# A second chunk that comes in halves, and casts moved to GpSimd, at the head of a graph layer

## The chip, the cores and the metric

The kernel runs on one core of one Trainium2 chip. The metric is the device time of one execution in microseconds (us). Each kernel was run several times and the median is compared.

## The reference

The inputs are x (8192 x 256, float32), a mostly empty adj (8192 x 8192, float32) and a weight (256 x 256, float32). One layer is computed:

```python
bw = sign(weight)
ba = maximum(sign(x), 0)
xw = ba @ bw.T                      # 8192 x 256
out = relu(adj @ xw)                # 8192 x 256, sum over 8192
result = layernorm(x + out)         # over the 256 features
```

Nearly all arithmetic and nearly all bytes (268 MB of adj) are in `adj @ xw`.

## The kernel before, in words

**Blocks, chunks, units.** The 8192 rows of adj are cut into 16 blocks of 512 rows. The sum over 8192 columns is cut into 8 chunks of 1024 columns. A chunk of one block is 2 MB and has 4 units, so a block has 32 units and the kernel 512. The units are numbered through: units 0 to 3 are the first chunk, 4 to 7 the second, unit 8 begins the third. TensorE needs the summed index on the partitions, so each unit is turned first.

**What happens to a unit.** VectorE turns it by 32x32 blocks (`turn`, L392), ScalarE makes a rounded copy `hi` of it (`make_hi`, L279), and then `lo`, the rest, is the turned unit minus `hi`. In "P" units GpSimd makes `lo` (L259, `turned` in SBUF); in "V" units VectorE does (`make_lo`, L396, `turned_v` in PSUM). Units 0, 1, 4 and 7 are V, units 2, 3, 5, 6, 8 and 9 are P. TensorE then multiplies `hi` and `lo` with `xw` and sums in PSUM (`use_unit`).

**The head: how xw is made.** During the first block xw is made too, in 16 groups of 4 steps of 128 rows of x; a chunk needs two groups, a group serves two units. For group g: x is cast to bf16 (`first_cast` L359 on VectorE for groups 0 and 1, `cast` L267 on ScalarE from group 2), TensorE transposes it (`turn_step`, L520), VectorE makes the step 0 or 1 (`make_step`, L365), TensorE multiplies with the signs of the weight (`make_xw`, L530), and the product is copied to SBUF (VectorE for group 0, L445; ScalarE's `copy_xw`, L272, for the others). TensorE's order is written out: transposes of group 0, product 0, transposes of group 1, then unit 0, product 1, transposes 2, unit 1, unit 2, product 2, transposes 3, units 3 and 4, product 3, transposes 4, units 5 and 6, and so on. A unit of a group waits until that group's product is copied.

**The first chunk in halves.** Units 0 to 3 hold half of the block's rows (256) and four steps, and not all 512 rows and two steps, so that unit 0 can start when half of the chunk has landed. Their products are 16 matmuls of 256 columns (L548) in place of 8 of 512 (L554). From unit 4 on a chunk is turned only when all of it has landed.

**The queues.** SyncE and ScalarE issue all loads, each two of the four quadrants of 32 partitions, each on its own queue. The issues of ScalarE stand in its program between its computing instructions: after `make_hi(n)` come the issues of x (L182) and adj (L168) that `x_at` and `issue_at` put at unit n, and after these, in the same pass, `copy_xw` and `cast`. The order on each queue is: weight, x for group 0, first half of chunk 0, x for group 1, its second half, then the two quadrants of x and of adj for the second chunk. Then, one quadrant at a time, x, adj, x, adj for each later chunk. SyncE issues the same at `units_turned` thresholds.

**What a first chunk's bytes are.** A chunk's x is 1.05 MB, a chunk of adj 2.10 MB, the weight 0.26 MB. Half of a first chunk is 1.05 MB, one group's x is 0.52 MB.

Of the kernel before, what the change touches and what calls it, by code (L numbers as in the profile page):

```python
# [5 lines left out]
Q = 32  # L6
G = P // Q
# [3 lines left out]
def build(nc, x, adj, w, out):  # L11
# [5 lines left out]
    NT = MB // Q  # L17
# [3 lines left out]
    SLOTS = 4  # L21
    CH = 8
    KC = N // CH
    KG = KC // G
    KB = KG // Q
# [3 lines left out]
    UPC = KB // UK  # L29
# [7 lines left out]
    GROUPS = CH * KB // GK  # L37
    UPG = GK // UK
    STEP_BUFS = 2
    BACK_AT = 4  # L40


# [15 lines left out]
        return before[kinds[n]][n]  # L58


    X_PIECES = [(0, GK), (GK, GK)] + [(c * KB, KB) for c in range(1, CH)]

    def piece_of_group(g):
        return g if g < KB // GK else g * GK // KB + 1

    adj_v = adj.rearrange("(b t i) (c g k) -> b c g i t k", t=NT, i=Q, c=CH, g=G)
    x_turn = x.rearrange("(c g b j) d -> c g j b d", c=CH, g=G, b=KB)
# [5 lines left out]
    with ctx:  # L73
# [3 lines left out]
        def sem(name):  # L77
            return ctx.enter_context(nc.semaphore(name))
# [39 lines left out]

        w_loaded = sem("w_loaded")
        x_loaded = [sem(f"x_loaded{i}") for i in range(len(X_PIECES))]  # L120
        halves_loaded = [sem(f"halves_loaded{i}") for i in range(2)]
        adj_loaded = [sem(f"adj_loaded{s}") for s in range(SLOTS)]
        rows_loaded = sem("rows_loaded")
        rows_stored = sem("rows_stored")
# [4 lines left out]
        signs_made = sem("signs_made")  # L129
        signs_turned = sem("signs_turned")  # L130
        signs_copied = sem("signs_copied")
        first_casts = sem("first_casts")
        casts_made = sem("casts_made")
        casts_turned = sem("casts_turned")
        steps_made = sem("steps_made")
# [27 lines left out]
        def raw_view(ch):  # L163
            return raw[:, ch % SLOTS, :].rearrange("p (t k) -> p t k", t=NT)
# [5 lines left out]

        def start_half(eng, i, quadrants):

            t0, t1 = i * NT // 2, (i + 1) * NT // 2
            for g in quadrants:
                eng.dma_start(raw_view(0)[g * Q:(g + 1) * Q, t0:t1],
                              adj_v[0, 0, g, :, t0:t1]).then_inc(halves_loaded[i], 16)

        def start_x(eng, i, quadrants):
            first, count = X_PIECES[i]
# [5 lines left out]


        def issue_at(ch, half):
            early = 4 + 2 * half if ch < CH else max(CH + 3 - ch, 0) + half
            return max(UPC * (ch - SLOTS + 1) + early, 0)

        def x_at(c, half):
            return max(UPC * c - 9 + 2 * half, 0)

        @block.sync
        def _(sp):
            sp.dma_start(w_sb[:, 0], w_rows[:, 0]).then_inc(w_loaded, 16)
            for i in range(2):
                start_x(sp, i, LOWER)
                start_half(sp, i, LOWER)

            def load_chunk(ch):
                if ch >= SLOTS:

                    sp.wait_ge(units_turned, (ch - SLOTS + 1) * UPC)
                start_chunk(sp, ch, LOWER)

            def store_rows(b):
                sp.wait_ge(blocks_done, b + 1)
                sp.dma_start(out_rows[b], rows[:]).then_inc(rows_stored, 16)

            def load_rows(b):
                if b == 0:

                    sp.wait_ge(xw_made, GROUPS)
                else:
                    sp.wait_ge(rows_stored, b * 16)
                sp.dma_start(rows[:], x_rows[b]).then_inc(rows_loaded, 16)

            start_x(sp, 2, LOWER)
            load_chunk(1)  # L220
            for c in range(2, CH):

                for half in range(2):
                    sp.wait_ge(units_turned, x_at(c, half) + 1)
                    start_x(sp, c + 1, LOWER[half:half + 1])
                    sp.wait_ge(units_turned, issue_at(c, half) + 1)
                    start_chunk(sp, c, LOWER[half:half + 1])
            for b in range(1, NBLK):
                for c in range(CH):
                    load_chunk(b * CH + c)  # L230
                    if c == 2 and b >= 2:
                        store_rows(b - 2)
                    if c == 3:
                        load_rows(b - 1)
            store_rows(NBLK - 2)
            load_rows(NBLK - 1)
            for b, ms in PIECES:
                if b == NBLK - 1:
                    sp.wait_ge(blocks_done, NBLK)
                else:  # L240
                    sp.wait_ge(last_piece_done, 1)
                sp.dma_start(out_rows[NBLK - 1, :, ms[0]:ms[-1] + 1],
                             rows[:, ms[0]:ms[-1] + 1]).then_inc(rows_stored, 16)
            sp.wait_ge(rows_stored, (NBLK - 1 + len(PIECES)) * 16)

        @block.gpsimd
        def _(pool):
            pool.memset(eps[:], EPS).then_inc(eps_set, 1)
            pool.memset(ident[:], 0.0).then_inc(zeroed, 1)
            pool.memset(ident_b[:], 0.0).then_inc(zeroed, 1)  # L250
            pool.wait_ge(zeroed, 2)
            for m in (ident, ident_b):
                pool.affine_select(out=m[:], in_=m[:], compare_op=ALU.not_equal, fill=1.0, base=0,
                                   pattern=[[-1, P]], channel_multiplier=1).then_inc(idents_made, 1)
            for n in range(UNITS):
                if kinds[n] == "P":

                    pool.wait_ge(his_made, n + 1)
                    pool.tensor_tensor(lo[:, n % RING], turned[:, ordinal(n) % TP], hi[:, n % RING].bitcast(f32),  # L259
                                       ALU.subtract).then_inc(p_los_made, 1)  # L260

        @block.scalar
        def _(act):
# [47 lines left out]
            start_half(act, 0, UPPER)  # L311
            act.wait_ge(eps_set, 1)
            act.activation(warm[:], eps[:], ACT.Copy)
            start_x(act, 1, UPPER)
            start_half(act, 1, UPPER)
            start_x(act, 2, UPPER)
            start_chunk(act, 1, UPPER)
            for n in range(UNITS):
                make_hi(n)
                for c in range(2, CH):  # L320
                    for half in range(2):
                        if n == x_at(c, half):
                            start_x(act, c + 1, UPPER[half:half + 1])
                for ch in range(2, NCHUNK):

                    for half in range(2):
                        if n == issue_at(ch, half):
                            start_chunk(act, ch, UPPER[half:half + 1])
                if n < UB:
                    g = n // UPG  # L330
                    if n % UPG and g >= 1:
                        copy_xw(g)
                    if n % UPG and g + 2 < GROUPS:
                        cast(g + 2)
                else:
                    ending(n // UB - 1, n % UB)
            act.wait_ge(relus_turned, (NBLK - 1) * MT)

# [11 lines left out]
        def _(dve):  # L350
# [3 lines left out]
            dve.scalar_tensor_tensor(out=sign_w[:], in0=w_sb, scalar=0.0, in1=w_neg,  # L354
                                     op0=ALU.is_gt, op1=ALU.subtract).then_inc(signs_made, 1)

            def first_cast(n):
                dve.wait_ge(x_loaded[n], G * 16)
                dve.tensor_copy(cast_x[:, n], x_sb[:, n * GK:(n + 1) * GK]).then_inc(first_casts, 1)  # L359

            def make_step(n):
                dve.wait_ge(casts_turned, n + 1)
                if n >= 2:
# [2 lines left out]

            def turn(n):
                ch, u = n // UPC, n % UPC
                if ch == 0:
                    if u < 2:  # L370
                        dve.wait_ge(halves_loaded[u], G * 16)
                elif u == 0:

                    dve.wait_ge(adj_loaded[ch % SLOTS], (ch // SLOTS + (ch % SLOTS > 0)) * G * 16)
                if kinds[n] == "P":
                    dst = turned[:, ordinal(n) % TP]
                    if ordinal(n) >= TP:
                        dve.wait_ge(p_los_made, ordinal(n) - TP + 1)
                else:
                    dst = turned_v  # L380
                    if n == 0:
                        dve.wait_ge(signs_copied, 1)
                    else:
                        dve.wait_ge(v_los_made, ordinal(n))
                src = raw[:, ch % SLOTS, :].rearrange("p (t k j) -> p k t j", t=NT, j=Q)
                if ch == 0:

                    g, t0 = u // UPG, u % UPG * NT // 2
                    uk, src = GK, src[:, g * GK:(g + 1) * GK, t0:t0 + NT // 2]
                else:  # L390
                    uk, src = UK, src[:, u * UK:(u + 1) * UK]
                dve.transpose(dst.rearrange("p (k t j) -> p k t j", k=uk, j=Q), src).then_inc(units_turned, 1)  # L392
# [43 lines left out]
                    make_shift(b, whole)  # L436


            first_cast(0)
            dve.wait_ge(signs_turned, 1)  # L440
            dve.tensor_copy(sign_wT[:], ps_wT).then_inc(signs_copied, 1)
            make_step(0)
            turn(0)
            dve.wait_ge(xw_made, 1)
            dve.tensor_copy(xw[:, 0:GK], ps_xw).then_inc(xw_copied, 1)  # L445
            first_cast(1)

            make_lo(0)
            make_step(1)
# [53 lines left out]
        def _(pe):  # L503
# [5 lines left out]
            last.then_inc(signs_turned, 1)  # L509

            def turn_step(n):
                if n < STEP_BUFS:
                    pe.wait_ge(first_casts, n + 1)
                else:
                    pe.wait_ge(casts_made, n - STEP_BUFS + 1)
                if n >= 2:
                    pe.wait_ge(steps_made, n - 1)
                for k in range(GK):
# [15 lines left out]
            def use_unit(n):  # L534
# [21 lines left out]
                                     start=(step == 0 and part is hi),  # L556
                                     stop=(step == last_step and part is lo))

                if n < UPC:
                    for k in range(GK):  # L560
                        for a in range(DH):
                            for part in (hi, lo):
# [114 lines left out]
```

## Time and profile before

| | |
|---|---|
| median of 3 runs | 992.87 us (991.89 to 993.97) |
| profiled execution, its own time | 991.81 us |
| span of its instructions | 989.9 us |
| TensorE busy | 972.1 us, 98% |
| GpSimd, VectorE, ScalarE busy | 839.8, 847.3, 613.5 us |
| loads and stores over the span | 297 GB/s read |

The span lies inside the profiled execution, 1.9 us shorter than its time. Engines are named PE (TensorE matmul), PEld (its weight loads), DVE (VectorE), ACT (ScalarE), POOL (GpSimd) and SP (SyncE); ACTq and SPq are the DMA issues that ACT's and SP's sequencers carry out. L12 is line 12 of the kernel. Times in rows are us from the span's start.

### The profile page before, as it was taken

How to read it: one execution, taken by the hardware profiler on the slowest of the kernel's cores; microseconds unless marked ns; L12 is line 12 of the kernel's file. 1: busy time of each engine (PE TensorE's matmuls, PEld its weight loads, DVE VectorE, ACT ScalarE, POOL GpSimd, SP SyncE). 2: the span in 40 equal slices, each digit the busy share in tenths (PEclk: the TensorE clock that was granted, in tenths of full speed). 3: DMA queues.
4: the chain of work that ended last, by engine and by line, in shares of the span. 5: the costliest groups of instructions: out<-in, count | busy, mean ns of one | idle time of the engine just before them, and what ended most of it. 6: DMA issues, size and time to landing. Idle time of an engine off the chain costs nothing.

```text
span 989.9 us, 12378 instructions
## 1 busy us (share of the span) xinstructions
PE 972.1 (98%) x4548; PEld 806.7 (81%) x4548; DVE 847.3 (86%) x879; ACT 613.5 (62%) x655; POOL 839.8 (85%) x360
## 2 busy tenths in 40 slices
PE   5999999999999999999999999999999999999997
PEld 4888888888888888888888888888888888888886
DVE  5868998989888898988989898898988989898894
ACT  3877675665656566565665656566565656656562
POOL 2567998988889889898998889899888998889893
PEclk9999999999999999999999999999999999999999
DMA  9999999999999999999999999999999999999971
GB/s 306 348 341 318 322 318 323 278 312 299 321 294 291 296 312 317 288 312 306 288 297 303 324 282 308 304 315 314 288 319 287 313 295 305 319 281 308 307 204 43
DMA packets 296428, 294.69 MB, mean 298 GB/s; under 512 B 9392, under 2 KB 296368, under 8 KB 296368
## 3 DMA queue, kind: packets, MB, share of 16 engines
q1 hardware_dynamic: 156640, 155.34, 57.2%
q10 hardware_dynamic: 139728, 138.56, 49.7%
q8 instruction: 36, 0.59, 0.3%
q14 instruction: 24, 0.20, 0.1%
HBM read 285.47 MB, written 8.39 MB: 297 GB/s over the span
## 4 chain that ended last, share of the span: by engine, by line
PE 97%; DVE 1%; DMA 1%; issue 0%; ACT 0%; ACTq 0%; DVEq 0%
PE ps L554 93%; PE ps L628 1%; PE ps L530 1%; DMA raw<-in_adj_dram 1%; PE ps L520 1%; PE ps L592 1%; PE ps L548 0%; ACTq L182 0%; DVE ps L392 0%; ACT hi L279 0%; DVE stats L404 0%; DVE rows L481 0%; PE ps L616 0%; DVE xw L445 0%; DVE lo L396 0%
## 5 line engine op out<-in xcount | busy, mean ns | idle before, releaser
L259 POOL TENSOR_TENSOR lo<-turned,hi 128x1024 fp32r<-128x1024 f32 x351 | 838.7, 2412 | 135.1 <-ACT hi L279 131.1
L554 PE MATMUL ps<-hi,xw 128*128 128x512 f32 x2016 | 787.1, 390 | 0.0
L554 PE MATMUL ps<-lo,xw 128*128 128x512 f32 x2016 | 784.7, 389 | 0.0
L279 ACT ACTIVATE hi<-turned 128x1024 fp32r<-128x1024 f32 x351 | 372.3, 1062 | 255.8 <-PE ps L554 173.6
L554 PEld LDWEIGHTS ps<-hi,xw 128*128 128x128 f32 x2016 | 378.5, 188 | 78.0
L554 PEld LDWEIGHTS ps<-lo,xw 128*128 128x128 f32 x2016 | 378.5, 188 | 77.9
L392 DVE STREAM_TRANSPOSE turned<-raw 128x1024 f32<-128x1024 f32 x351 | 425.1, 1218 | 0.0
L396 DVE TENSOR_TENSOR lo<-ps,hi 128x1024 fp32r<-128x1024 f32 x161 | 196.5, 1220 | 106.3 <-ACT hi L279 106.3
L279 ACT ACTIVATE hi<-ps 128x1024 fp32r<-128x1024 f32 x161 | 165.1, 1026 | 89.9 <-PE ps L554 77.2
L392 DVE STREAM_TRANSPOSE ps<-raw 128x1024 f32<-128x1024 f32 x161 | 196.2, 1219 | 3.8 <-DMA raw<-in_adj_dram 3.8
L296 ACT ACTIVATE rows<-rows,shift,rstd 128x256 f32<-128x256 f32 x62 | 36.3, 586 | 0.6 <-DVE shift L415 0.6
L365 DVE TENSOR_SCALAR rows<-ps 128x1024 bf16<-128x1024 bf16 x16 | 10.9, 679 | 14.1 <-PE ps L520 14.1
L404 DVE BATCH_NORM_STATS2 stats<-rows 128x6 f32<-128x256 f32 x64 | 22.4, 412 | 0.1
L272 ACT ACTIVATE xw<-ps 128x1024 fp32r<-128x1024 f32 x15 | 15.4, 1024 | 10.5 <-PE ps L530 8.4
L530 PE MATMUL ps<-sign_wT,rows 128*128 128x256 bf16 x128 | 18.1, 288 | 0.9 <-DVE rows L365 0.9
L400 DVE TENSOR_TENSOR rows<-ps,rows 128x1024 f32<-128x1024 f32 x15 | 18.0, 1199 | 0.0
L530 PEld LDWEIGHTS ps<-sign_wT,rows 128*128 128x128 bf16 x128 | 11.8, 103 | 6.2 <-issue 4.5
L267 ACT ACTIVATE relu<-x_sb 128x1024 bf16<-128x1024 f32 x14 | 14.7, 1050 | 2.6 <-DMA x_sb<-in_x_dram 2.6
L288 ACT ACTIVATE relu<-ps 128x512 f32<-128x512 f32 x30 | 16.0, 584 | 0.0
L628 PEld LDWEIGHTS ps<-ident,relu 128*128 128x128 f32 x120 | 14.0, 140 | 2.0
L628 PE MATMUL ps<-ident,relu 128*128 128x128 f32 x120 | 15.5, 272 | 0.0
L520 PE MATMUL ps<-ident_b,relu 128*128 128x128 bf16 x128 | 10.6, 230 | 3.5 <-DVE relu L359 3.5
(38 smaller groups left out, 109.8 us busy)
## 6 DMA issues: line engine op xcount, KB each, us to landing
raw<-in_adj_dram SPq DMA_DIRECT2D x254, 512.0 KB, 11.1
raw<-in_adj_dram ACTq DMA_DIRECT2D x254, 512.0 KB, 12.0
rows<-in_x_dram SPq DMA_DIRECT2D x16, 512.0 KB, 10.7
out_dram<-rows SPq DMA_DIRECT2D x15, 512.0 KB, 15.8
x_sb<-in_x_dram SPq DMA_DIRECT2D x14, 256.0 KB, 10.2
x_sb<-in_x_dram ACTq DMA_DIRECT2D x14, 256.0 KB, 11.9
raw<-in_adj_dram SPq DMA_DIRECT2D x4, 256.0 KB, 7.0
raw<-in_adj_dram ACTq DMA_DIRECT2D x4, 256.0 KB, 7.8
```

The lines of the kernel that those rows point to most:

```text
L259: pool.tensor_tensor(lo[:, n % RING], turned[:, ordinal(n) % TP], hi[:, n % RING].bitcast(f32), ALU.subtract).then_inc(p_los_made, 1)
L279: act.activation(hi[:, n % RING], src, ACT.Copy).then_inc(his_made, 1)
L288: act.activation(relu[:, a], acc[b % 2][a], ACT.Relu).then_inc(relus_made, 1)
L296: done = act.activation(rows[:, m], rows[:, m], ACT.Identity, bias=shift[:, m:m + 1], scale=rstd[:, m:m + 1])
L392: dve.transpose(dst.rearrange("p (k t j) -> p k t j", k=uk, j=Q), src).then_inc(units_turned, 1)
L396: dve.tensor_tensor(lo[:, n % RING], turned_v[:, :], hi[:, n % RING].bitcast(f32), ALU.subtract).then_inc(v_los_made, 1)
L400: dve.tensor_tensor(rows[:, ms], back[:, ms], rows[:, ms], ALU.add).then_inc(sums_made, 1)
L404: dve.bn_stats(stats[:, m], rows[:, m]).then_inc(stats_made, 1)
L520: last = pe.transpose(ps_xT[n % 2][:, k, i], cast_x[:, n % STEP_BUFS, k, i * P:(i + 1) * P], ident_b[:])
L530: last = pe.matmul(ps_xw[:, k], step_xT[:, n % 2, k, i], sign_wT[:, i], start=(i == 0), stop=(i == DH - 1))
L554: return pe.matmul(acc[b % 2][a], xw[:, step, a * P:(a + 1) * P], part[:, n % RING, k * MB:(k + 1) * MB], start=(step == 0 and part is hi) ...
L628: last = pe.transpose(back[:, m, a * P:(a + 1) * P], relu[:, a, m * P:(m + 1) * P], ident[:])
```

## The change

The second chunk is loaded in halves of its rows too, and its x in two groups of 0.52 MB. Units 4 to 7 become units of half the rows and four steps, like units 0 to 3. Group 0 is cast by VectorE as before, groups 1 and 2 are cast by GpSimd, the others by ScalarE. Product 0 is copied by ScalarE. ScalarE copies products 0 to 3 right after `make_hi` of units 0, 2, 4 and 6 (the products before: at units 3, 5, 7), and both `copy_xw` and `cast` now come ahead of the DMA issues of the same unit. The last half of the second chunk is issued after the first unit is turned, and the quadrants of later chunks one unit later than before.

```diff
+    EARLY_CASTS = 3
...
-    X_PIECES = [(0, GK), (GK, GK)] + [(c * KB, KB) for c in range(1, CH)]
+    HALVED = 2
+    X_PIECES = [(g * GK, GK) for g in range(HALVED * UPC // UPG)] + [(c * KB, KB) for c in range(HALVED, CH)]
...
         def issue_at(ch, half):
-            early = 4 + 2 * half if ch < CH else max(CH + 3 - ch, 0) + half
+            early = 5 + 2 * half if ch < CH else max(CH + 3 - ch, 0) + half
...
         def x_at(c, half):
-            return max(UPC * c - 9 + 2 * half, 0)
+            return UPC * (c - HALVED) + 2 * half
...
-            for i in range(2):
+            for i in range(2 * HALVED):
                 start_x(sp, i, LOWER)
-                start_half(sp, i, LOWER)
+                if i < 2 * HALVED - 1:
+                    start_half(sp, i, LOWER)
+
+            sp.wait_ge(units_turned, 1)
+            start_half(sp, 2 * HALVED - 1, LOWER)
...
-            start_x(sp, 2, LOWER)
-            load_chunk(1)
...
+            for g in range(1, EARLY_CASTS):
+                pool.wait_ge(x_loaded[g], G * 16)
+                if g >= STEP_BUFS:
+                    pool.wait_ge(casts_turned, g - STEP_BUFS + 1)
+                pool.tensor_copy(cast_x[:, g % STEP_BUFS], x_sb[:, g * GK:(g + 1) * GK]).then_inc(pool_casts, 1)
...
-            start_x(act, 1, UPPER)
-            start_half(act, 1, UPPER)
-            start_x(act, 2, UPPER)
-            start_chunk(act, 1, UPPER)
+            for i in range(1, 2 * HALVED):
+                start_x(act, i, UPPER)
+                if i < 2 * HALVED - 1:
+                    start_half(act, i, UPPER)
             for n in range(UNITS):
                 make_hi(n)
+                if n < UB:
+                    g = n // UPG
+                    if n % UPG == (0 if g < HALVED * UPC // UPG else 1):
+                        copy_xw(g)
+                    if n % UPG and EARLY_CASTS <= g + 2 < GROUPS:
+                        cast(g + 2)
+                if n == 0:
+                    start_half(act, 2 * HALVED - 1, UPPER)
...
-                if n < UB:
-                    g = n // UPG
-                    if n % UPG and g >= 1:
-                        copy_xw(g)
-                    if n % UPG and g + 2 < GROUPS:
-                        cast(g + 2)
...
-                if ch == 0:
+                if ch < HALVED:
                     if u < 2:
-                        dve.wait_ge(halves_loaded[u], G * 16)
+                        dve.wait_ge(halves_loaded[2 * ch + u], G * 16)
...
-            first_cast(0)
+            dve.wait_ge(x_loaded[0], G * 16)
+            dve.tensor_copy(cast_x[:, 0], x_sb[:, 0:GK]).then_inc(first_cast, 1)
...
             turn(0)
-            dve.wait_ge(xw_made, 1)
-            dve.tensor_copy(xw[:, 0:GK], ps_xw).then_inc(xw_copied, 1)
-            first_cast(1)
...
-                if n < UPC:
+                if n < HALVED * UPC:
                     for k in range(GK):
```

## Rows read from the trace of the kernel before

**Rows 1.** The page: busy time by engine, and the chain that ended last.
```profile
PE 972.1 (98%) x4548; PEld 806.7 (81%) x4548; DVE 847.3 (86%) x879; ACT 613.5 (62%) x655; POOL 839.8 (85%) x360
...
PE 97%; DVE 1%; DMA 1%; issue 0%; ACT 0%; ACTq 0%; DVEq 0%
```
**Rows 2.** Waits of PE: us in total, times, longest.
```profile
PE ps L548 <- ACT xw L272: 2.2, 1, 2.2
```
**Rows 3.** Busy time by stretch: length, PE, PEld, DVE, ACT, POOL, PEclk, DMA, GB/s.
```profile
80.00:970.00 890.00, 890.00 (x4012) 737.75 (x4011) 783.97 (x803) 556.99 (x596) 794.03 (x333) 1.00 1.09 301
```
**Rows 4.** Timeline of ACT: start, us, instruction, idle before it.
```profile
15.97 1.74 ACTq L182 DMA_DIRECT2D x_sb<-in_x_dram  x1
...
19.44 3.36 ACTq L182 DMA_DIRECT2D x_sb<-in_x_dram  x1
...
22.85 1.02 ACT L272 ACTIVATE xw<-ps 128x1024 fp32r<-128x1024 f32 x1 [2.08 <-issue]
...
29.49 1.06 ACT L267 ACTIVATE relu<-x_sb 128x1024 bf16<-128x1024 f32 x1 [1.26 <-DMA x_sb<-in_x_dram]
...
30.45 1.04 ACT L279 ACTIVATE hi<-turned 128x1024 fp32r<-128x1024 f32 x1
```
**Rows 5.** The chain that ended last, in order of time: start, us, what.
```profile
26.10 0.89 PE ps L530 x8
26.99 0.45 PE ps L520 x8
27.44 1.96 PE ps L548 x16
29.40 1.84 PE ps L554 x8
```
**Rows 6.** Timeline of DVE, early.
```profile
12.26 0.68 DVE L359 CAST relu<-x_sb 128x1024 bf16<-128x1024 f32 x1
12.86 1.22 DVE L396 TENSOR_TENSOR lo<-ps,hi 128x1024 fp32r<-128x1024 f32 x1
...
33.30 1.25 DVE L392 STREAM_TRANSPOSE turned<-raw 128x1024 f32<-128x1024 f32 x1
```
**Rows 7.** Timeline of POOL, early.
```profile
1.35 0.29 POOL L253 TENSOR_SCALAR_AFFINE_SELECT ident<-ident 128x128 f32<-128x128 f32 x1 [0.24 <-POOL ident_b L250]
...
19.90 4.71 POOL L259 TENSOR_TENSOR lo<-turned,hi 128x1024 fp32r<-128x1024 f32 x2 [18.01 <-ACT hi L279]
...
31.57 2.39 POOL L259 TENSOR_TENSOR lo<-turned,hi 128x1024 fp32r<-128x1024 f32 x1 [2.14 <-ACT hi L279]
35.72 4.76 POOL L259 TENSOR_TENSOR lo<-turned,hi 128x1024 fp32r<-128x1024 f32 x2 [1.76 <-ACT hi L279]
```
**Rows 8.** Issue to landing: x of group 1 (issued 3.1 to 3.6), x at 16.0, adj at 17.9.
```profile
DMA to landing us min/median/max: 6.5/6.8/7.7
...
DMA to landing us min/median/max: 12.5/13.0/13.5
...
DMA to landing us min/median/max: 15.4/15.4/15.4
```
**Rows 9.** Timeline of PE: units 0 and 1's work, unit 6's and 8's first matmul.
```profile
14.23 0.55 PE L548 MATMUL ps<-hi,xw 128*128 128x256 f32 x1 [0.19 <-DVE lo L396]
...
19.56 0.36 PE L548 MATMUL ps<-hi,xw 128*128 128x256 f32 x1
...
34.31 0.40 PE L554 MATMUL ps<-hi,xw 128*128 128x512 f32 x1
...
39.37 0.40 PE L554 MATMUL ps<-hi,xw 128*128 128x512 f32 x1
```
**Rows 10.** Busy time by stretch, from the start to three landings (columns as Rows 3).
```profile
0.00:17.80 17.80, 8.09 (x45) 6.44 (x45) 10.76 (x13) 3.53 (x4) 1.12 (x9) 1.00 0.95 289
0.00:23.49 23.49, 12.01 (x76) 9.86 (x76) 13.05 (x15) 7.13 (x8) 4.71 (x11) 1.00 0.99 303
0.00:29.45 29.45, 17.54 (x125) 15.23 (x126) 19.00 (x21) 11.54 (x12) 8.23 (x12) 1.00 1.01 312
```

More of the change, by code:

```diff
@@ L58, in ordinal, with piece_of_chunk @@
         return before[kinds[n]][n]
-    X_PIECES = [(0, GK), (GK, GK)] + [(c * KB, KB) for c in range(1, CH)]
+    HALVED = 2
+    X_PIECES = [(g * GK, GK) for g in range(HALVED * UPC // UPG)] + [(c * KB, KB) for c in range(HALVED, CH)]
     def piece_of_group(g):
-        return g if g < KB // GK else g * GK // KB + 1
+        return [i for i, (first, count) in enumerate(X_PIECES) if first <= g * GK < first + count][0]
+    def piece_of_chunk(c):
+        return X_PIECES.index((c * KB, KB))
     adj_v = adj.rearrange("(b t i) (c g k) -> b c g i t k", t=NT, i=Q, c=CH, g=G)
@@ L120, in build @@
         x_loaded = [sem(f"x_loaded{i}") for i in range(len(X_PIECES))]
-        halves_loaded = [sem(f"halves_loaded{i}") for i in range(2)]
+        halves_loaded = [sem(f"halves_loaded{i}") for i in range(2 * HALVED)]
         adj_loaded = [sem(f"adj_loaded{s}") for s in range(SLOTS)]
@@ L131, in build @@
         signs_copied = sem("signs_copied")
-        first_casts = sem("first_casts")
+        first_cast = sem("first_cast")
+        pool_casts = sem("pool_casts")
         casts_made = sem("casts_made")
@@ L171, in start_half @@
         def start_half(eng, i, quadrants):
-            t0, t1 = i * NT // 2, (i + 1) * NT // 2
+            ch, t0 = i // 2, i % 2 * NT // 2
             for g in quadrants:
-                eng.dma_start(raw_view(0)[g * Q:(g + 1) * Q, t0:t1],
-                              adj_v[0, 0, g, :, t0:t1]).then_inc(halves_loaded[i], 16)
+                eng.dma_start(raw_view(ch)[g * Q:(g + 1) * Q, t0:t0 + NT // 2],
+                              adj_v[0, ch, g, :, t0:t0 + NT // 2]).then_inc(halves_loaded[i], 16)
         def start_x(eng, i, quadrants):
@@ L217, in load_rows @@
                 sp.dma_start(rows[:], x_rows[b]).then_inc(rows_loaded, 16)
-            start_x(sp, 2, LOWER)
-            load_chunk(1)
-            for c in range(2, CH):
+            for c in range(HALVED, CH):
                 for half in range(2):
                     sp.wait_ge(units_turned, x_at(c, half) + 1)
-                    start_x(sp, c + 1, LOWER[half:half + 1])
+                    start_x(sp, piece_of_chunk(c), LOWER[half:half + 1])
                     sp.wait_ge(units_turned, issue_at(c, half) + 1)
@@ L313, in _ @@
             act.activation(warm[:], eps[:], ACT.Copy)
-            start_x(act, 1, UPPER)
-            start_half(act, 1, UPPER)
-            start_x(act, 2, UPPER)
-            start_chunk(act, 1, UPPER)
+            for i in range(1, 2 * HALVED):
+                start_x(act, i, UPPER)
+                if i < 2 * HALVED - 1:
+                    start_half(act, i, UPPER)
             for n in range(UNITS):
                 make_hi(n)
-                for c in range(2, CH):
+                if n < UB:
[6 more added lines that the diff above has]
+                    start_half(act, 2 * HALVED - 1, UPPER)
+                for c in range(HALVED, CH):
                     for half in range(2):
                         if n == x_at(c, half):
-                            start_x(act, c + 1, UPPER[half:half + 1])
+                            start_x(act, piece_of_chunk(c), UPPER[half:half + 1])
                 for ch in range(2, NCHUNK):
@@ L328, in _ @@
                             start_chunk(act, ch, UPPER[half:half + 1])
-                if n < UB:
-                    g = n // UPG
-                    if n % UPG and g >= 1:
-                        copy_xw(g)
-                    if n % UPG and g + 2 < GROUPS:
-                        cast(g + 2)
-                else:
+                if n >= UB:
                     ending(n // UB - 1, n % UB)
@@ L355, in _ @@
                                      op0=ALU.is_gt, op1=ALU.subtract).then_inc(signs_made, 1)
-            def first_cast(n):
-                dve.wait_ge(x_loaded[n], G * 16)
-                dve.tensor_copy(cast_x[:, n], x_sb[:, n * GK:(n + 1) * GK]).then_inc(first_casts, 1)
             def make_step(n):
@@ L368, in turn @@
                 ch, u = n // UPC, n % UPC
-                if ch == 0:
+                if ch < HALVED:
                     if u < 2:
-                        dve.wait_ge(halves_loaded[u], G * 16)
+                        dve.wait_ge(halves_loaded[2 * ch + u], G * 16)
                 elif u == 0:
-                    dve.wait_ge(adj_loaded[ch % SLOTS], (ch // SLOTS + (ch % SLOTS > 0)) * G * 16)
+                    dve.wait_ge(adj_loaded[ch % SLOTS], (ch // SLOTS + (ch % SLOTS >= HALVED)) * G * 16)
                 if kinds[n] == "P":
@@ L385, in turn @@
                 src = raw[:, ch % SLOTS, :].rearrange("p (t k j) -> p k t j", t=NT, j=Q)
-                if ch == 0:
+                if ch < HALVED:
                     g, t0 = u // UPG, u % UPG * NT // 2
@@ L511, in turn_step @@
             def turn_step(n):
-                if n < STEP_BUFS:
-                    pe.wait_ge(first_casts, n + 1)
+                if n == 0:
+                    pe.wait_ge(first_cast, 1)
+                elif n < EARLY_CASTS:
+                    pe.wait_ge(pool_casts, n)
                 else:
-                    pe.wait_ge(casts_made, n - STEP_BUFS + 1)
+                    pe.wait_ge(casts_made, n - EARLY_CASTS + 1)
                 if n >= 2:
```

## The prediction

> **What bounds the kernel now.** The page comes first. TensorE is busy 972.1 of 989.9 us, and 97% of the chain that ended last is its own work [rows 1]. The stretches say where the rest is: from 80 to 970 us it is busy 890.00 of 890.00 us [rows 3]. So an edit of the first 40 us can only move the moment from which TensorE never waits again. I look for that moment in TensorE's waits. After its first unit there is one wait, 2.2 us, for ScalarE's copy of product 1 [rows 2]. ScalarE's timeline shows why the copy was late: an issue of x began at 19.44, held ScalarE's sequencer for 3.36 us, and the copy behind it started at 22.85 after 2.08 us of "issue" [rows 4]. The change plainly removes this wait, since the copy now comes ahead of the issues. The question is what is late next.
>
> **What lies close behind the wait.** Two more things on ScalarE and GpSimd run in the shadow of those 2.2 us. ScalarE's cast of group 4 waited for x of the third chunk until 29.49. `make_hi` of unit 6 stands behind this cast in ScalarE's program and began at 30.45 [rows 4]. GpSimd's `lo` of unit 6 ran from 31.57 for 2.39 us, to 33.96 [rows 7]. TensorE began unit 6 at 34.31 [rows 9]. So unit 6 had 0.35 us in hand, less than a sixth of the wait that goes. This chain begins at a landing, and the change leaves cast 4 where it was, behind `make_hi(5)` and ahead of `make_hi(6)`.
>
> **When that landing comes.** Here I compare bytes moved with bytes queued up to a landing. At 17.8 us 289 GB/s had moved 5.14 MB (x of the second chunk ends at 0.26 + 3.15 + 1.05 = 4.46 MB of the order). At 23.49, when the second chunk was in, it was 7.12 MB (6.55 in the order). At 29.45 it was 9.19 MB; x of the third chunk ends at 6.55 + 0.52 + 1.05 + 0.52 = 8.65 MB [rows 10]. The lead is 0.68, 0.57 and 0.54 MB: landings follow bytes moved, at (9.19 - 7.12) / 5.96 us = 347 GB/s between the last two. The delay from issue to landing is no constant: 7.7 us for an x issue at 3.6, 13.5 for one at 16.0 [rows 8], as the backlog grew. The change reorders bytes only within the second chunk; from x of the third chunk on the order is x, adj, x, adj as before. So x of the third chunk still lands at 29.5, provided no queue runs empty. By the same rule the new pieces land so: first half of the second chunk (4.98 MB + 0.6) at 19.1, its second half at 23.5.
>
> **The change part by part.**
>
> *Copy 0 and cast 1 leave VectorE.* `make_lo(0)` then waits only for `make_hi(0)`, which ends at 12.2; it started at 12.86 behind a cast of 0.68 us [rows 6]. Gain 0.6 us. Copy 0 on ScalarE takes 1.02 us [rows 4], done by 13.3, beside it.
>
> *Casts 1 and 2 on GpSimd.* The trace shows no cast there. From below: 0.29 us, an operation with one input on 128 columns; from above: 2.40 us, half of 4.76, the operation with two inputs on the same 1024 columns [rows 7]. I take the upper, which has the right size. x of group 1 has landed by 3.6 + 7.7 = 11.3 [rows 8]. So the cast ends at 13.7, the transposes of group 1 take about 1.1 us at the slow start, and unit 0 starts at 14.9 (at 13.6, set by `lo`, if the cast takes less than about 1.2). It was 14.23 [rows 9]. From the first matmul of unit 0 to that of unit 1 took 19.56 - 14.23 = 5.33 us, with product 1 and the transposes of group 2 [rows 9]. A half unit is 1.96, a product 0.89, the transposes 0.45 [rows 5]. Without waits unit 6 would start after that, units 1 to 5 (9.80), products 2 and 3 and transposes 3 and 4 (2.68): 17.8 us after unit 0, at 31.4 to 32.7. Both ends lie ahead of 33.96, so the cast's price is hidden.
>
> *Second chunk in halves.* Unit 4 no longer waits for the whole chunk, but `make_lo(4)` stands behind `turn(5)`, which waits for the second half at 23.5. It ends near 25.9, as needed. Price: 1.96 - 1.84 = 0.12 us for each of units 4 to 7 [rows 5]. Units 4 and 5 pay it while TensorE would wait anyway, units 6 and 7 on the path: +0.24 us.
>
> *The wait that takes the place of the old one.* Transposes 4 need cast 4, which ends at 29.49 + 1.06 = 30.55 [rows 4]; then 0.45 + 1.96 bring unit 6 to 33.0 at the earliest, and its `lo` to 33.96. So unit 6 starts at 34.0, not 34.31: -0.31 us. TensorE will wait 0.3 to 1.3 us before transposes 4 and 1 us before unit 6, where it waited 2.2 us earlier.
>
> *Issues one unit later, and behind copies.* Behind the waiting copies and casts on ScalarE stand the issues of its queue. The tightest is x of the fourth chunk and then adj, the latter behind cast 4, at about 29.5. By then ScalarE's queue has been given 5.0 MB and has moved about half of 9.19, 4.6, or a little less. It has 0.4 to 0.6 MB left, over 2 us of work at half of 347 GB/s, so it stays fed, and I cost this at nothing. If this cover went, adj of the fourth chunk would be late; its units are three further on. `turn(8)` ran at 33.30 with adj issued at 17.9 and 15.4 us to landing, so on landing [rows 6, 8]; that too stays.
>
> *Sum.* -0.31 + 0.24 = -0.07, say -0.1 us at unit 8 (39.3 for 39.37) and from there to the end. The profiled execution's 991.81 (span 989.9 and 1.9 around it) would become 991.7. It lay 1.06 under the median of the runs, so the median becomes 992.87 - 0.1 = **992.8 us**.
>
> **The rivals.** 0.2% (2.0 us) is about what a measurement of this kernel can tell from no change.
>
> *Landings come earlier.* SyncE's half of that x landed after 12.5 us, at 28.5, ScalarE's at 29.5 [rows 8]. Were they even, or less held up by full queues, x could land 0.5 to 1 us earlier and unit 6 with it. Unit 8 bounds this. Its `lo` ends at 35.72 + 2.4 = 38.1 [rows 7] and follows the landing of adj at 33.3; unit 8 started at 39.37 [rows 9]. So with adj unmoved at most 1.25 us come: 991.6 to 992.3, still "same". Chance 0.12. With both landings early by over a microsecond the whole wait would come back: 34.31 - 31.4 - 0.24 = 2.7 us, 990.2. Chance 0.07; the steady 347 GB/s speaks against it.
>
> *The other side: the delay from issue counts.* ScalarE's second x issue of the third chunk was at 15.97 [rows 4]. Now it stands behind copy 1, which waits for product 1 on TensorE, at 18.4 to 19.9. If 13.5 us from issue still held, x would land at 31.9 to 33.4 and unit 6 would start 2.4 to 3.9 us later than at 34.0: 995.2 to 996.7. It decides from a landing at 31.6 on. Against it stand the bytes [rows 10]. It needs an empty queue. Chance 0.05.
>
> *GpSimd's cast is slow.* Unit 0 may start up to 34.0 - 17.8 = 16.2 without harm, so the cast may take 16.2 - 1.1 - 11.3 = 3.8 us. Beyond it each microsecond costs one. At three times a `lo` (7.2 us) that is +3.3: 996.2. Against it: the first `lo` of all began right when `hi` was there, and the first two took 4.71 us, later two 4.76 [rows 7]; no first use was dear. Chance 0.04. The Trainium skill (GPSIMD Engine Reference, section Instruction dispatch) says that the first call to a freshly loaded GpSimd kernel pays about 6 us more. An estimate by that page is a cast of 2.4 + 6 = 8.4 us, and then 4.5 us slower. By that rule the first `lo` should have shown it too; the trace has no such gap, so I leave it its small chance.
>
> **Chances.** Forecast (within a few tenths of 992.8) 0.72; earlier x alone 0.12; everything earlier 0.07; later landings 0.05; slow cast 0.04. Faster by over 0.2%: 0.07. Within: 0.72 + 0.12 = 0.84. Slower: 0.09. The range reaches down to the case of the earlier x with some spread of the median, 991.2, and up by a microsecond, the spread of the runs shown, 993.9.
>
> **What would show it.** Right: TensorE's wait for L272 gone, two new waits near 30 and 33 us, on L267 and on L259; cast 4 waiting for x until about 29.5; unit 8 starting near 39.3; GpSimd's casts between 0.3 and 2.4 us. Wrong: cast 4 starting before 28.5 or after 30, any wait of TensorE beyond 40 us, a GpSimd cast over 3.8 us, or a queue that runs empty.

## The result, and the profile after

The changed kernel takes 1004.31 us (median of 6 runs, 998.12 to 1011.44), the kernel before 993.42 us (median of 6, 991.89 to 994.34). The ratio is 1.0113, with a 95% interval of 1.0067 to 1.0159. It is 1.1% slower, outside the range of the prediction, and its runs lie 13 us apart where those of before lie within 2.5 us; why they scatter so is not shown. Ratios here and below are of the means of the runs, the times are medians. The profiled execution took 1000.46 us, with a span of 998.7 us, so the rows below show one of the milder cases: 8.8 us more span.

Busy time by engine and the chain that ended last, on the page of the kernel after, answer to [rows 1]:

```profile
PE 974.7 (98%) x4580; PEld 807.9 (81%) x4580; DVE 845.7 (85%) x877; ACT 612.5 (61%) x655; POOL 841.9 (84%) x362
...
PE 90%; DMA 7%; issue 1%; DVE 0%; ACT 0%; POOL 0%; ACTq 0%; DVEq 0%; POOLq 0%
```

The busy time of TensorE is 2.6 us longer, and the other 6 us of the loss are waits. The halves explain a small part of the 2.6 us: e3 below keeps them and has 972.5 us. Where the rest comes from stays open. Transfers are 7% of the chain, where they were 1%. TensorE's waits from 0 to 110 us (engine, line, what it waited for, us in total, times, longest):

```profile
PE ps L533 <- ACT relu L281: 4.5, 5, 1.8
PE ps L567 <- POOL lo L273: 2.9, 3, 1.0
PE ps L533 <- POOL relu L268: 2.2, 1, 2.2
...
PE ps L567 <- ACT xw L286: 0.3, 1, 0.3
```

The wait of [rows 2] for the copy is gone, as the change intends. In its place TensorE waits five times for a cast of x on ScalarE and three times for a `lo` behind one. By unit 8, where the forecast stopped, little of the loss is there. Its first matmul starts at 39.89, against 39.37 before and 39.3 foretold:

```profile
39.89 0.40 PE L567 MATMUL ps<-hi,xw 128*128 128x512 f32 x1
```

ScalarE's timeline of the kernel after answers to [rows 4]:

```profile
23.80 0.32 ACTq L189 DMA_DIRECT2D x_sb<-in_x_dram  x1
25.00 1.06 ACT L293 ACTIVATE hi<-turned 128x1024 fp32r<-128x1024 f32 x1 [0.18 <-DVE turned L405]
29.99 1.06 ACT L281 ACTIVATE relu<-x_sb 128x1024 bf16<-128x1024 f32 x1 [3.93 <-DMA x_sb<-in_x_dram]
30.00 0.32 ACTq L175 DMA_DIRECT2D raw<-in_adj_dram  x1
30.47 0.39 ACTq L189 DMA_DIRECT2D x_sb<-in_x_dram  x1
30.95 1.04 ACT L293 ACTIVATE hi<-turned 128x1024 fp32r<-128x1024 f32 x1
...
40.45 1.06 ACT L281 ACTIVATE relu<-x_sb 128x1024 bf16<-128x1024 f32 x1 [1.74 <-DMA x_sb<-in_x_dram]
40.46 0.32 ACTq L175 DMA_DIRECT2D raw<-in_adj_dram  x1
...
52.37 1.06 ACT L281 ACTIVATE relu<-x_sb 128x1024 bf16<-128x1024 f32 x1 [2.80 <-DMA x_sb<-in_x_dram]
52.38 0.32 ACTq L175 DMA_DIRECT2D raw<-in_adj_dram  x1
```

Cast 4 waits until 29.99 (foretold: 29.5). Directly behind it, at 30.00, comes an adj issue that the kernel before made at 24.79, well ahead of its cast 4:

```profile
24.79 0.36 ACTq L168 DMA_DIRECT2D raw<-in_adj_dram  x1
```

Between the issues of 23.80 and 30.00 ScalarE issues nothing. The stretches of the kernel after (columns as in [rows 3]; the last number is GB/s) show what follows:

```profile
31.00:32.00 1.00, 0.90 (x12) 0.90 (x13) 0.24 (x1) 1.00 (x3) 0.00 (x0) 1.00 1.11 350
32.00:33.00 1.00, 1.00 (x11) 1.00 (x10) 0.45 (x1) 1.00 (x2) 0.93 (x1) 1.00 1.14 317
33.00:34.00 1.00, 0.68 (x6) 0.48 (x4) 0.93 (x1) 1.00 (x2) 1.00 (x1) 1.00 1.10 212
34.00:35.00 1.00, 0.39 (x3) 0.42 (x4) 1.00 (x2) 1.00 (x2) 0.46 (x1) 1.00 1.15 211
35.00:36.00 1.00, 1.00 (x11) 1.00 (x10) 1.00 (x2) 0.71 (x1) 0.21 (x1) 1.00 1.08 254
```

The rate falls from 350 to 211 GB/s, while the DMA share stays at 1.10 or more: that column alone would have hidden it. The queues of the kernel after (packets, MB, share of 16 engines) at 31 to 32, 33 to 34 and 35 to 36 us:

```profile
q10 hardware_dynamic: 181, 0.18, 56.0%
q1 hardware_dynamic: 174, 0.17, 55.1%
...
q1 hardware_dynamic: 196, 0.20, 104.2%
q10 hardware_dynamic: 13, 0.01, 6.3%
...
q10 hardware_dynamic: 127, 0.13, 54.9%
q1 hardware_dynamic: 129, 0.12, 53.6%
```

q10, by the times ScalarE's queue, runs all but dry after 32 us and flows again after 35. The two issues of 30.00 and 30.47 do not help it for about 5 us. SyncE's queue, with the other almost dry, moves 0.20 MB in a microsecond, where the two together move 0.35. Later SyncE's queue runs dry too: it issues nothing from 40.00 to 46.48, and from 49 to 51 us q1 moves 0.05 MB and q10 0.38. The rate stays low over most of block 0. From 55 to 65 us, first before and then after:

```profile
55.00:65.00 10.00, 10.00 (x65) 8.14 (x64) 6.94 (x8) 7.81 (x9) 7.03 (x4) 1.00 1.10 348
```

```profile
55.00:65.00 10.00, 9.00 (x53) 6.73 (x51) 6.46 (x6) 5.29 (x6) 6.61 (x3) 1.00 1.12 241
```

Five times in block 0 the same loop goes round. The chain of the kernel after, in order of time:

```profile
30.47 9.96 DMA x_sb<-in_x_dram
...
40.90 11.45 DMA x_sb<-in_x_dram
...
52.82 12.24 DMA x_sb<-in_x_dram
...
65.53 11.64 DMA x_sb<-in_x_dram
...
77.64 11.97 DMA x_sb<-in_x_dram
```

A cast waits for x; behind the cast stand the issue of the next adj and of the next x; that x lands 10 to 12 us later, and the next even cast waits for it. The even casts began at 29.99, then 40.45, 52.37, 65.08, 77.19 and 89.64: 59.65 us for five chunks, 11.9 each. In the kernel before cast 4 began at 29.49 and cast 14 at 79.09, without a wait for x, 49.6 us for the same five:

```profile
79.09 1.04 ACT L267 ACTIVATE relu<-x_sb 128x1024 bf16<-128x1024 f32 x1
```

### The profile page after: what moved, and what is told of

Read it like the earlier page. It is cut to its first block, busy times and chain, and to the rows that moved or that the text cites. A ratio compares the mean times of both kernels' runs of the same rounds, so it can differ in the third digit from the quotient of the medians.

```text
span 998.7 us, 12450 instructions
## 1 busy us (share of the span) xinstructions
PE 974.7 (98%) x4580; PEld 807.9 (81%) x4580; DVE 845.7 (85%) x877; ACT 612.5 (61%) x655; POOL 841.9 (84%) x362
## 3 DMA queue, kind: packets, MB, share of 16 engines
q10 hardware_dynamic: 139792, 138.56, 49.6%
## 4 chain that ended last, share of the span: by engine, by line
PE 90%; DMA 7%; issue 1%; DVE 0%; ACT 0%; POOL 0%; ACTq 0%; DVEq 0%; POOLq 0%
PE ps L567 88%; DMA x_sb<-in_x_dram 7%; PE ps L641 1%; PE ps L605 1%; PE ps L561 0%; PE ps L543 0%; ACT relu L281 0%; ACTq L175 0%; DVE stats L417 0%; PE ps L533 0%; DVE rows L492 0%; PE ps L629 0%; POOL relu L268 0%; ACT xw L286 0%; DVE mv L420 0%
## 5 line engine op out<-in xcount | busy, mean ns | idle before, releaser
L561 PE MATMUL ps<-hi,xw 128*128 128x256 f32 x64 | 17.6, 309 | 1.0 <-POOL lo L273 0.9
L561 PE MATMUL ps<-lo,xw 128*128 128x256 f32 x64 | 17.0, 299 | 0.0
L533 PEld LDWEIGHTS ps<-ident_b,relu 128*128 128x128 bf16 x128 | 8.6, 103 | 10.4 <-ACT relu L281 5.9
```

What stands on the lines that cost most here:

```text
L533: last = pe.transpose(ps_xT[n % 2][:, k, i], cast_x[:, n % STEP_BUFS, k, i * P:(i + 1) * P], ident_b[:])
L561: return pe.matmul(acc[b % 2][a][:, n0:n0 + MB // 2], xw[:, step, a * P:(a + 1) * P], part[:, n % RING, k * MB // 2:(k + 1) * MB // 2], st ...
```

## The experiments

Each run below leaves the computation whole. A is the theory of the dry queue behind a waiting cast, B is that the issues simply come a unit too late, C is that the halves cost it.

**e1: the kernel after with the issue times of before.**

```diff
-            early = 5 + 2 * half if ch < CH else max(CH + 3 - ch, 0) + half
+            early = 4 + 2 * half if ch < CH else max(CH + 3 - ch, 0) + half
...
-            return UPC * (c - HALVED) + 2 * half
+            return max(UPC * c - 9 + 2 * half, 0)
```

> The kernel after, with only the issue times of the kernel before (x and adj of later chunks one unit earlier). Theory A (ScalarE's issues stand behind a cast that waits for a landing, and its queue runs dry): one adj quadrant now comes ahead of cast 4, at about 24 us, but x and the next adj still stand behind it, at 30; the queue just runs out when they begin to flow, so part of the loss stays: 993 to 997 us. Theory B (the issues come one unit too late, wherever they stand): the whole loss goes, 992 to 993.5 us. Theory C (the halves of the second chunk, with their smaller transfers and matmuls, cost it): nothing changes, 1000 us or more.

Measured: 992.8 us against 993.6, ratio 0.9993 (0.9984 to 1.0001). The whole loss is gone, more than A as first put had allowed. This run alone fits B.

**e2: the kernel after with ScalarE's casts behind the issues of their unit.**

```diff
-                    if n % UPG and EARLY_CASTS <= g + 2 < GROUPS:
-                        cast(g + 2)
...
                         if n == issue_at(ch, half):
                             start_chunk(act, ch, UPPER[half:half + 1])
+                if n < UB and n % UPG and EARLY_CASTS <= g + 2 < GROUPS:
+                    cast(g + 2)
```

> The kernel after, with ScalarE's casts moved behind the issues of the same unit; the issue times stay one unit later. Theory A: ScalarE's queue no longer runs dry behind a waiting cast, 992 to 994 us. Theory B: the loss stays in most part, above 997 us. Theory C: 1000 us or more.

Measured: 993.19 against 993.6 us, ratio 1.0001 (0.9991 to 1.0011); one of the twelve runs took 997.48. Here every issue still comes a unit late, so B falls; and in e1 the issues still stand behind the casts, so the place alone is not enough either. What e1 and e2 share at cast 4 is one transfer: the first adj quadrant of the fourth chunk, 0.52 MB, is issued by ScalarE ahead of the cast. ScalarE's issue, first of e1 and then of e2:

```profile
24.88 0.32 ACTq L175 DMA_DIRECT2D raw<-in_adj_dram  x1
```

```profile
25.48 0.36 ACTq L175 DMA_DIRECT2D raw<-in_adj_dram  x1
```

The stretch of the dry queue, first of e1 and then of e2:

```profile
32.00:35.00 3.00, 2.07 (x18) 1.90 (x17) 2.46 (x3) 3.00 (x5) 2.39 (x1) 1.00 1.10 348
```

```profile
32.00:35.00 3.00, 2.07 (x18) 1.90 (x17) 2.37 (x3) 3.00 (x5) 2.39 (x1) 1.00 1.10 347
```

Theory A2: both moves together put that quadrant, and its like in each later chunk, behind the waiting cast.

**e3: both edits.** The diffs of e1 and e2 together.

> Both edits: issue times of the kernel before, and ScalarE's casts behind the issues of their unit; halves, GpSimd's casts and the early copies stay. Theories A and B: 992 to 993.3 us, equal to the kernel before or a few tenths under it, since x of the third chunk still lands near 29.5 us. Theory C: 1000 us or more.

Measured: 992.69 against 993.6 us, ratio 0.9999 (0.9984 to 1.0013); one of the eleven runs took 1000.68, and no profile shows why. Halves, GpSimd's casts and the early copies stay, and together they cost or bring at most 0.16%. C falls.

**e4: the kernel before with `copy_xw` ahead of the issues of its unit.**

```diff
                 make_hi(n)
+                if n < UB and n % UPG and n // UPG >= 1:
+                    copy_xw(n // UPG)
...
-                    if n % UPG and g >= 1:
-                        copy_xw(g)
```

> The kernel before, with only copy_xw moved ahead of the issues of its unit. By the chain of cast 4, make_hi(6) and lo(6), the wait of 2.2 us for the copy goes and all but 0.35 us of it comes back before unit 6: 0.3 us faster, 993.1 against 993.4. Rival, that the wait was the only one: 2.2 us faster. Theory A adds that an issue behind a copy that waits costs nothing as long as the queue holds several microseconds of work.

Measured: 993.07 against 993.6 us, ratio 0.9996 (0.9988 to 1.0005). The rival, that all 2.2 us are gained, lies outside the interval. This is the prediction's step from the copy to unit 6 by itself. First two rows of ScalarE's timeline in e4, then its chain at unit 6 (start, us, what):

```profile
20.82 1.00 ACT L272 ACTIVATE xw<-ps 128x1024 fp32r<-128x1024 f32 x1
...
30.16 1.06 ACT L267 ACTIVATE relu<-x_sb 128x1024 bf16<-128x1024 f32 x1 [2.17 <-DMA x_sb<-in_x_dram]
```

```profile
32.24 2.40 POOL lo L259
34.64 0.14 issue
34.78 2.08 PE ps L554 x8
```

Copy 1 runs at 20.82 in place of 22.85, and the 2 us come back whole: cast 4 waits for x, `lo` of unit 6 ends at 34.64 and TensorE begins the unit behind it.

**e5: the kernel before with the two moves of the change alone.** Issue times one unit later, ScalarE's `copy_xw` and `cast` ahead of the issues; no halves, no cast on GpSimd.

```diff
-            early = 4 + 2 * half if ch < CH else max(CH + 3 - ch, 0) + half
+            early = 5 + 2 * half if ch < CH else max(CH + 3 - ch, 0) + half
...
-            return max(UPC * c - 9 + 2 * half, 0)
+            return UPC * (c - 2) + 2 * half
...
                 make_hi(n)
+                if n < UB:
+                    g = n // UPG
+                    if n % UPG and g >= 1:
+                        copy_xw(g)
+                    if n % UPG and g + 2 < GROUPS:
+                        cast(g + 2)
```

> The kernel before, with two moves of the change alone: issues of later chunks one unit later, and ScalarE's copy and cast ahead of the issues of their unit. No halves in the second chunk, no cast on GpSimd. Theory A2 (these two together put one adj quadrant behind cast 4, from about 25 to 30 us, and ScalarE's queue needs it some 5 us before it is empty): the loss is there, 998 to 1010 us, with stretches near 210 GB/s. Theory C (halves): 993 us.

Measured: 1001.47 against 993.5 us, ratio 1.0073 (1.0049 to 1.0097). These two moves make a loss of this kind. Whether they make all of it isn't resolved, 0.73% for 1.13% with intervals that overlap. The profiled execution is the slowest of the six, 1004.77 us. Its queues from 33 to 35 us:

```profile
q1 hardware_dynamic: 412, 0.41, 106.3%
q10 hardware_dynamic: 30, 0.02, 6.9%
```

**e6: the kernel after with SyncE's issues one unit earlier.**

```diff
-                    sp.wait_ge(units_turned, x_at(c, half) + 1)
+                    sp.wait_ge(units_turned, max(x_at(c, half), 1))
...
-                    sp.wait_ge(units_turned, issue_at(c, half) + 1)
+                    sp.wait_ge(units_turned, max(issue_at(c, half), 1))
```

> The kernel after, with only SyncE's issues one unit earlier, ScalarE's unchanged. Theory A2 (ScalarE's queue runs out first, SyncE's only as a consequence): most of the loss stays, 998 us or more, and the first slow stretch is at 32 to 35 us as before. Theory B2 (both queues together are short): below 996 us.

Measured: 1002.06 against 993.5 us, ratio 1.0091 (1.0071 to 1.0111). Earlier issues on SyncE's queue do not help, while e2, which edits ScalarE's program alone, removes the loss: the cause is on ScalarE's. I had expected the slow stretch at 32 to 35 us as before. The slow stretch came about 1 us later (236 GB/s at 34 to 35 us, 199 at 35 to 36), with cast 4 at 31.50.

**e9: the kernel after with one single issue moved ahead of cast 4.**

```diff
+                    if n == issue_at(3, 0):
+                        start_chunk(act, 3, UPPER[0:1])
                     if n % UPG and EARLY_CASTS <= g + 2 < GROUPS:
                         cast(g + 2)
...
-                        if n == issue_at(ch, half):
+                        if n == issue_at(ch, half) and (ch, half) != (3, 0):
```

> The kernel after, with one single issue of ScalarE moved: the first adj quadrant of the fourth chunk comes ahead of cast 4 (near 25 us) and not behind it (30 us). The same stands behind casts 6, 8, 10, 12 and 14 still. Theory F (the first dry stretch starts it, and each late landing makes the next cast late and with it the next issues): ScalarE's queue holds a quadrant more at 30 us, the stretch of 32 to 35 us stays near 348 GB/s and most or all of the loss goes, 992 to 996 us. Theory G (each chunk makes its own dry stretch, whatever came before): only the first of six goes, 1000 us or more.

Measured: 999.27 against 993.7 us, ratio 1.0068 (1.0054 to 1.0082). The stretches of e9, columns as before:

```profile
32.00:35.00 3.00, 2.12 (x19) 1.92 (x16) 2.25 (x3) 3.00 (x4) 2.40 (x1) 1.00 1.10 347
42.00:44.00 2.00, 2.00 (x20) 1.68 (x19) 1.00 (x2) 1.14 (x2) 1.52 (x1) 1.00 1.11 223
```

The first dry stretch is gone with the one transfer, as A2 says. But the next comes at 42 us, behind cast 6. So a chunk makes its own (theory G), and the first is not what starts them all; F falls. The time lies between the two forecasts, 0.7 us under the 1000 of G. The loss is 0.68% for 1.13%, and the intervals overlap, so how much went with the one transfer is not resolved.

**e7: e3, and both quadrants of a chunk's x ahead of its adj.**

```diff
-            return max(UPC * c - 9 + 2 * half, 0)
+            return max(UPC * c - 9, 0)
...
+                sp.wait_ge(units_turned, x_at(c, 0) + 1)
+                start_x(sp, piece_of_chunk(c), LOWER)
                 for half in range(2):
-                    sp.wait_ge(units_turned, x_at(c, half) + 1)
-                    start_x(sp, piece_of_chunk(c), LOWER[half:half + 1])
```

> As e3 (old issue times, casts behind the issues), and both quadrants of a chunk's x issued ahead of its adj. If the bytes ahead of it set when x lands, x of the third chunk (7.6 MB and a lead of 0.6) lands near 26.5 us in place of 30, cast 4 holds nobody up, and unit 8 is bound by the landing of adj at 33.3 us: it starts 1 to 1.2 us ahead of the 39.37 us of the kernel before, 992.4 against 993.6 us. Rival, that the delay from issue counts: no gain, 993 us or more.

Measured: 991.81 against 993.5 us, ratio 0.9985 (0.9976 to 0.9994). Cast 4 no longer holds anybody up: it ran at 28.52 without a wait for x. The profile of e7 shows the new bound, and not the gain that I expected of it. Its chain:

```profile
18.70 15.06 DMA raw<-in_adj_dram
...
33.79 1.25 DVE turned L405
...
38.30 1.01 ACT xw L286
39.31 0.04 issue
39.35 2.11 PE ps L567 x8
```

adj of the third chunk lands at 33.8, and unit 8 starts at 39.35, as in the kernel before (39.37). The time is 0.15% lower all the same; this execution (991.87 us, beside 991.81 for that of the kernel before) is no witness for where that comes from, and it stays open.

**e8: e4, and both quadrants of a chunk's x ahead of its adj.** The same edit on the kernel before; no halves, no cast on GpSimd.

> As e4 (the kernel before with copy_xw first), and both quadrants of a chunk's x ahead of its adj; whole second chunk, no cast on GpSimd. It tells what the halves are worth once x comes early: unit 4 then still waits for the whole second chunk at 23.5 us and its lo, near 27 us, where TensorE could be there near 25; the gain against the kernel before is that of e7 or a few tenths of a microsecond more (no dearer matmuls): 992.2 to 992.8 us.

Measured: 991.7 against 993.5 us, ratio 0.9981 (0.9973 to 0.999). It is faster than the kernel before by 0.19%, more than I had expected, and no slower than e7, so the second chunk's halves and GpSimd's casts bring nothing that shows even then. Its profiled span is 989.1 us, 0.8 us under the 989.9 of before. The whole of it is there at unit 8, which starts here, in place of at 39.37:

```profile
38.56 0.40 PE L554 MATMUL ps<-hi,xw 128*128 128x512 f32 x1
```

This is the version to keep.

## Why the prediction was wrong

**Right.** What the change removes went, and the chain behind it was the right one: cast 4 at 29.99 (29.5 foretold), two new waits of TensorE, GpSimd's cast at 1.04 us (between 0.29 and 2.40). The 0.24 us put down for the halves are too small for these runs to show. The 0.3 us of gain at unit 6 did not come: it started at 34.61, with cast 4 half a microsecond late (34.31 before, 34.0 foretold). Two of the signs named for a wrong forecast did come: a queue that runs empty, and waits of TensorE beyond 40 us. The experiment e4 shows the step by itself: without the copy's wait unit 6 waits for its `lo`, and nothing is gained. The rule that landings follow bytes moved held roughly where both queues were full: when x of the third chunk had landed, ScalarE's queue had moved 4.56 MB before, 4.66 MB after and 4.80 MB in e6, where that was at 31.5 us. The spread of 0.24 MB is 1.4 us of that queue's work at half of 347 GB/s, so the rule is no finer than that. And x moved ahead of one adj quadrant on each queue (e7, e8) came in time.

**The step that failed** is the one on the issues that stand behind copies: "It has 0.4 to 0.6 MB left, over 2 us of work at half of 347 GB/s, so it stays fed, and I cost this at nothing." The backlog was right: the queue worked until 32 to 33 us, about 2.5 us after cast 4 began. What I set beside it was wrong. I took it that an issue of 29.5 flows when the queue comes to it. The profile after shows 5.3 us from the issue at 30.00 until the queue moves again. So a backlog of 2.5 us is 2.8 us too little; in these the kernel moves about 0.14 MB less in a microsecond (0.35 less 0.21), some 0.4 MB, over 1 us of transfer at the full rate. I had priced it once and as zero. It comes again with later chunks of block 0: 11.9 us between even casts for 9.9 before, five times, 10 us, and 8.8 us of span.

**The rival that came nearest** was the one of later landings (0.05), and it had the place but not the mechanism. x of the third chunk, on which I made it turn, landed in time. It was x of the fourth, fifth and later chunks. I had stopped looking at unit 8 "and from there to the end", because TensorE had never waited there. That had been true only while casts found their x landed, or nearly: in the kernel before cast 6 waited 0.51 us for it.

**Two moves, neither harmful alone.** e1 undoes the one, e2 the other, and each brings it back within the interval; e5 makes a loss from the two. An edit-by-edit sum, each costed with the rest as it was, cannot find this.

## What to carry to other kernels

An issue that stands behind an instruction that waits for a landing closes a loop: landing, cast, issue, landing. Compare what is left in the queue at that moment with the time from an issue to the first byte and not with zero, and do it for every turn of the loop, not for the first. When a wait on a compute engine goes, look for DMA issues behind the next waiting instruction on the same engine; and judge by the GB/s of short stretches and by the packets of each queue, since the busy share stayed at 1.1 while the rate fell by two fifths, from 350 to 211 GB/s.

## What the runs showed of the hardware that I had not expected

- With the other queue almost dry, one queue moved about 200 GB/s (0.20 MB from 33 to 34 us, 0.19 MB from 50 to 51 us), with both full 345 to 351, transfers of the same kind. The busy share was about 1.1 in both.
- From an issue on a queue about to run dry until it moved again: about 5 us (ScalarE's, issued at 30.00, back after 35 us; SyncE's, issued at 46.48, back after 51 us). At the start of the kernel before, transfers of x issued at 1.2 us had landed whole after 3.1 to 3.6 us. So it is not a fixed price of an empty queue; which of the traffic, the other queue or the number of transfers makes it longer was not tried.
- A GpSimd cast of 128x1024 from float32 to bf16 took 1.04 us, its subtraction with two inputs 2.40 us. The first cast was no longer than the second, and began as its x landed. By the Trainium skill (GPSIMD Engine Reference, section Instruction dispatch) it might have paid about 6 us; none shows in its own time. GpSimd stood idle for 9.74 us before it, and whether something was loaded then, no run here tells.
- In e6 TensorE did nothing from 30 to 32 us, and its granted clock was 0.50 (1.2 GHz) from 33 to 35 us. In the kernel before it kept 1.00 over its idle 2.2 us. What decides between the two was not tried. The stretches of e6:

```profile
30.00:32.00 2.00, 0.00 (x0) 0.00 (x0) 0.00 (x0) 0.51 (x1) 0.00 (x0) 1.00 1.10 346
32.00:33.00 1.00, 0.39 (x4) 0.40 (x5) 0.00 (x0) 1.00 (x2) 0.00 (x0) 0.75 1.12 334
33.00:34.00 1.00, 1.00 (x9) 1.00 (x8) 0.32 (x1) 1.00 (x2) 0.43 (x1) 0.50 1.13 266
```
